# A streamed factorization-machine kernel: the columns in blocks of 512, 384 and 128 instead of 512, 352 and 160

## The reference

```python
x_reg = input_data @ W_lin.T + b_lin
emb = input_data @ factors                                   # 12500 x 16
sum_squared = jnp.square(emb.sum(axis=1))
squared_sum = (jnp.square(input_data) @ jnp.square(factors)).sum(axis=1)
h = jax.nn.relu(emb @ W1.T + b1)                             # 128
h = jax.nn.relu(h @ W2.T + b2)                               # 64
dnn_out = h @ W3.T + b3
x = x_reg + 0.5 * (sum_squared - squared_sum)[:, None] + dnn_out
x = 0.5 + jax.nn.sigmoid(x) * 5.0
```

## Time and profile before

| | |
|---|---|
| median of three runs | 133.88 us |
| time of the profiled execution | 133.76 us |
| its span in the trace | 132.0 us |
| TensorE busy (PE) | 107.0 us, 81% |
| ACT busy | 61.5 us, 47% |
| DVE busy | 52.6 us, 40% |
| DMA | 52.36 MB, mean 397 GB/s |
| chain that ended last | DMA 54%, PE 40% |

### The profile page before, as it was taken

The page is one execution under the profiler, slowest core; times in us unless marked ns, Lnnn a source line. Parts: engine busy times, 40 slices in busy tenths (PEclk is TensorE's granted clock), DMA queues, the critical chain, the costliest instruction groups (busy, mean ns, idle before and its releaser), DMA issues.

```text
span 132.0 us, 2607 instructions
## 1 busy us (share of the span) xinstructions
PE 107.0 (81%) x1123; PEld 34.6 (26%) x1123; DVE 52.6 (40%) x51; ACT 61.5 (47%) x52; POOL 15.7 (12%) x48
## 2 busy tenths in 40 slices
PE   6099969429979839749749979999998987989992
PEld 4012222002212112112112233322222112345881
DVE  0391063027036036046045016565351351576571
ACT  4030067029039039049048046868562561465851
POOL 3015000200010200200200110164530000000000
PEclk9999999995999999999977999999999999999999
DMA  3999899989999998998999999899999999999700
GB/s 106 413 531 417 377 477 472 407 387 467 427 387 462 457 427 387 457 437 387 467 457 427 387 457 447 377 432 412 452 407 407 462 415 417 418 404 411 302 26 1
DMA packets 3489, 52.36 MB, mean 397 GB/s; under 512 B 404, under 2 KB 536, under 8 KB 1560
## 3 DMA queue, kind: packets, MB, share of 16 engines
q1 hardware_dynamic: 3480, 52.23, 93.2%
HBM read 52.22 MB, written 0.00 MB: 396 GB/s over the span
## 4 chain that ended last, share of the span: by engine, by line
DMA 54%; PE 40%; SPq 2%; DVE 1%; issue 1%; ACT 1%
DMA xr<-in_x_pairs 43%; PE p_lin L506 34%; DMA xr<-in_x_end 11%; PE p_sq L506 2%; PE p_h L601 2%; SPq L273 1%; PE p_tot L506 1%; PE p_h L632 1%; PE p_tot L614 0%; DVE h L454 0%; DVE h L449 0%; SPq L267 0%; SPq L266 0%; PE p_tot L621 0%; SPq L265 0%
## 5 line engine op out<-in xcount | busy, mean ns | idle before, releaser
L327 ACT ACTIVATE sq<-xr 128x2560 f32<-128x2560 f32 x20 | 45.9, 2333 | 46.8 <-DMA xr<-in_x_pairs 38.8
L427 DVE TENSOR_TENSOR sq<-xr 128x1536 f32<-128x1536 f32 x20 | 34.6, 1761 | 53.7 <-DMA xr<-in_x_pairs 42.9
L506 PE MATMUL p_lin<-xr,wr 128*17 128x512 f32 x320 | 39.9, 638 | 15.6 <-DMA xr<-in_x_pairs 14.4
L506 PE MATMUL p_lin<-sq,wz 128*18 128x512 f32 x320 | 37.7, 592 | 0.0
L506 PEld LDWEIGHTS p_lin<-xr,wr 128*17 128x17 f32 x320 | 9.2, 102 | 44.5 <-issue 38.4
L307 POOL COPY wr<-hd 128x136 f32 (+1 forms) x20 | 9.3, 464 | 75.0 <-PE p_lin L506 75.0
L506 PEld LDWEIGHTS p_lin<-sq,wz 128*18 128x18 f32 x320 | 10.1, 98 | 25.8 <-issue 25.0
L506 PE MATMUL p_lin<-xr,hd 128*17 128x352 f32 (+1 forms) x128 | 10.0, 380 | 1.3 <-DMA xr<-in_x_end 1.3
L437 DVE TENSOR_TENSOR sq<-xr 128x1408 f32<-128x1408 f32 (+3 forms) x6 | 6.6, 1135 | 6.1 <-DMA xr<-in_x_end 6.1
L337 ACT ACTIVATE sq<-xr 128x1408 f32<-128x1408 f32 (+3 forms) x6 | 5.7, 983 | 6.3 <-DMA xr<-in_x_end 6.3
L506 PE MATMUL p_lin<-sq,ws 128*18 128x352 f32 x64 | 6.6, 459 | 0.0
(11 more groups left out here) (52 smaller groups left out, 40.8 us busy)
## 6 DMA issues: line engine op xcount, KB each, us to landing
xr<-in_x_pairs SPq DMA_DIRECT2D x8, 4096.0 KB, 21.9
xr<-in_x_groups SPq DMA_DIRECT2D x4, 2048.0 KB, 18.3
xr<-in_x_end SPq DMA_DIRECT2D x1, 2112.0 KB, 10.5
xr<-in_x_end SPq DMA_DIRECT2D x3, 640.0 KB, 12.0
xr<-in_x_end SPq DMA_DIRECT2D x1, 1760.0 KB, 14.3
xr<-in_x_end SPq DMA_DIRECT2D x1, 1056.0 KB, 12.4
hd<-in_head SPq DMA_DIRECT2D x1, 952.0 KB, 4.8
xr<-in_x_end SPq DMA_DIRECT2D x1, 704.0 KB, 13.7
```

The costliest lines, as they stand in the source:

```text
L327: nc.scalar.activation(sq[:, ring(s), BY_DVE:CHUNKS, :], xr[:, s, BY_DVE:CHUNKS, :], ACT.Square).then_inc(act_squared, 1)
L427: nc.vector.tensor_tensor(sq[:, ring(s), 0:BY_DVE, :], xr[:, s, 0:BY_DVE, :], xr[:, s, 0:BY_DVE, :], ALU.mult).then_inc(dve_squared, 1)
L506: return nc.tensor.matmul(out, lhsT, rhs, start=False, stop=False, skip_group_check=True)
```

## The change

The columns are cut into 512, 384 and 128. The first two blocks are now both done in 12 groups of 8 chunks; the groups of block 1 are 384 wide (1.57 MB), ten of them loaded as five pairs and two singly. Block 2 is 128 wide and is done over all 96 chunks in eight pieces of 24, 20, 16, 12, 8, 8, 6 and 2 chunks. In block 1 the products take their weights from the resident tables (`w`, and `ws`, which grows from 32 to 96 chunks), so POOL copies no weights there. Block 1 is closed in one go between its last group and the first piece of block 2. The bytes loaded are the same, and so is the number of products times their columns.

```diff
-ENDS = 32
+ENDS = ALL - 1
-TOTAL = 2 * GROUPS - END_GROUPS
-PAIRED = 16
+TOTAL = 2 * GROUPS
+PAIRED = TOTAL - TWO
-BLOCKS = ((0, 512), (512, 352), (864, 160))
+BLOCKS = ((0, 512), (512, 384), (512 + 384, 128))
-PIECES = ((1, 0, (4, 2), (4, 2)), (1, 12, (4, 1), (4, 1)), (1, 22, (3,), (3,)), (1, 28, (2,), (2,)),
-          (2, 0, (2, 2), (2, 2)), (2, 8, (2, 2), (2, 2)), (2, 16, (2, 2), (2, 2)), (2, 24, (2, 1), (2, 1)),
-          (2, 30, (1,), (1,)))
+PIECES = ((0, (7, 6), (6, 5)), (24, (6, 5), (5, 4)), (44, (5, 4), (4, 3)), (60, (4, 3), (3, 2)),
+          (72, (2, 2), (2, 2)), (80, (2, 2), (2, 2)), (88, (2, 1), (2, 1)), (94, (1,), (1,)))
...
+        def slots_free(i):
+
+            return TOTAL - SLOTS + TWO * ((ends_at(i) - 1) // (TWO * SLOT) + 1)
...
+                    sp.dma_start(group_chunks(TWO * p, 0, TWO * CHUNKS),
+                                 x_pairs1[p - GROUPS // TWO, :, 0:TWO * CHUNKS * WIDTH]
+                                 ).then_inc(x_landed[at // TWO], 16)
...
-            for g in range(GROUPS, TOTAL):
-                place(g, g, 1 + CHUNKS * (g - GROUPS))
...
+            act.wait_ge(sq_used, RING + TOTAL)
             copy_lin(1, 0)
             copy_lin(1, 1)
             nc.scalar.copy(rest[:, :], p_lin[1][:, BLOCKS[1][1]:HALF]).then_inc(rest_copied, 1)
             embedding_square(1)
-            square_end(4, 1)
             layer1(1, BLOCKS[1][1])
...
+            square_end(0, 0)
+            square_end(0, 1)
             sigmoid(1)
+            for i in range(1, len(PIECES)):
+                for j in range(len(PIECES[i][1])):
+                    square_end(i, j)
...
+            layer2(1)
             square_end(0, 0)
             square_end(0, 1)
+            scale(1)
+            for i in range(1, LAST_PIECE):
+                for j in range(len(PIECES[i][2])):
+                    square_end(i, j)
...
+            def multiply1(g):
+                c0 = CHUNKS * (g - GROUPS)
+                for c in range(CHUNKS):
+                    add_mm(quad(p_lin[1], c, LIN, 0, WIDTH), w[:, 1 + c0 + c, :], group_chunks(g, c, 1))
...
             first_layer(p_h1[0], BLOCKS[1][1], lin[:, cols(1)]).then_inc(p_h1_done[1], 1)
             linear(1)
             embedding_square(1)
-            multiply_end(5)
-            dve_squares_end(5, 0)
             pe.wait_ge(h1a_ready[1], 1)
             layer2(1)
-            act_squares_end(4, 1)
-            multiply_end(6)
...
+            multiply_end(0)
             layer3(1)
-            add_squares_end(6)
+            add_squares_end(0)
+            for i in range(1, LAST_PIECE - 1):
+                multiply_end(i)
+                add_squares_end(i)
+            multiply_end(LAST_PIECE - 1)
+            multiply_end(LAST_PIECE).then_inc(p_lin_done, 1)
+            add_squares_end(LAST_PIECE - 1)
             pe.wait_ge(lin_ready[2], 1)
 
             pe.wait_ge(h1b_ready[0], 1)
             first_layer(p_h1[1], BLOCKS[2][1], lin[:, cols(2)]).then_inc(p_h1_done[2], 1)
-            add_squares_end(7)
 
             pe.wait_ge(sg_ready[0], 1)
             embedding_sum(2)
-            add_squares_end(8).then_inc(squares_done, 1)
+            add_squares_end(LAST_PIECE).then_inc(squares_done, 1)
```

More of the change, by code:

```diff
@@ L203, in tot_bank, with group, group_chunks, group_squares @@
             return p_tot[k % 2]
[L205 to L225, removed]
+        x_row = xr[:, :].rearrange("p s c b -> p (s c b)")
+        sq_row = sq[:, :].rearrange("p s c b -> p (s c b)")
+        SLOT = CHUNKS * HALF
+        WIDTH = BLOCKS[1][1]
+        LAST_WIDTH = BLOCKS[LAST][1]
+        def group(g):
+            return TWO * SLOT * (g // TWO % (SLOTS // TWO)) + g % TWO * CHUNKS * WIDTH
+        def group_chunks(g, c, n):
+            at = group(g) + c * WIDTH
+            return x_row[:, at:at + n * WIDTH]
+        def group_squares(g, c, n):
+            at = SLOT * ring(g) + c * WIDTH
+            return sq_row[:, at:at + n * WIDTH]
+        def piece(c, n):
+            return x_row[:, c * LAST_WIDTH:(c + n) * LAST_WIDTH]
+        IN_RING = PIECES[4][0]
+        LAST_PIECE = len(PIECES) - 1
+        def squared_piece(c, n):
+            if c < IN_RING:
+                return sq_row[:, c * LAST_WIDTH:(c + n) * LAST_WIDTH]
+            at = group(PAIRED) + (c - IN_RING) * LAST_WIDTH
+            return x_row[:, at:at + n * LAST_WIDTH]
         def ring(s):
@@ L256, in act_count, with dve_count @@
         def act_count(i, j):
+            return sum(len(q[1]) for q in PIECES[:i]) + j + 1
+        def dve_count(i, j):
             return sum(len(q[2]) for q in PIECES[:i]) + j + 1
-        def dve_count(i, j):
-            return sum(len(q[3]) for q in PIECES[:i]) + j + 1
         @block.sync
@@ L647, in _ @@
                 for s in range(0, SLOTS, TWO):
-                    pair(r, s, 0)
+                    landed(pe, r, s)
+                    multiply(r, s, 0)
+                    multiply(r, s + 1, 0)
+                    add_squares(r, s, 0)
+                    add_squares(r, s + 1, 0)
             layer1(0)
@@ L658, in _ @@
             layer3(0)
+            pe.wait_ge(ws_ready, 2)
             for g in range(GROUPS, PAIRED, TWO):
-                pair(g // SLOTS, g % SLOTS, 1)
+                landed(pe, g // SLOTS, g % SLOTS)
+                multiply1(g)
+                multiply1(g + 1)
+                add_squares1(g)
+                add_squares1(g + 1)
             for g in range(PAIRED, TOTAL):
                 single(pe, g)
[L664 to L672, removed]
-            multiply_end(4)
-            act_squares_end(4, 0)
-            dve_squares_end(4, 0)
-            dve_squares_end(4, 1)
+                multiply1(g)
+                add_squares1(g)
             pe.wait_ge(lin_ready[1], 2)
@@ L762 @@
     params[:, C_B3] = np.asarray(L0_rec_b3)
-    arrays = {"head": head, "x_first": x_first, "x_rest": x_rest, "x_pairs": x_pairs, "x_groups": x_groups, "x_end": x_end}
+    arrays = {"head": head, "x_first": x_first, "x_rest": x_rest, "x_pairs": pairs[0], "x_pairs1": pairs[1],
+              "x_groups": x_groups, "x_end": x_end}
     nc = bacc.Bacc("TRN2", target_bir_lowering=False, num_devices=1)
```

180 lines of the change are left out of this document (75 added, 105 removed).

## The result

The changed kernel takes 137.61 us (median of four runs, 137.27 to 140.73) against 133.84: the ratio is 1.027, 95% interval 1.024 to 1.031. It is slower, as forecast, but by 3.8 us where 0.85 were forecast, and it lies above the range of 133.7 to 136.3. One of the four runs (140.73) was in a slower state that some executions of any kernel show; the ratio leaves it out. The profiled execution took 137.27 us against 133.76, its span is 135.5.

The account below looks back on a forecast made before the run. The DMA stream (54% of the chain) was taken to bound the kernel, TensorE (40%) close behind. Block 2's addition +0.98 and tail -0.13 gave +0.85 on 133.76: 134.6, or 134.7 by the median; range 133.7 to 136.3 us.

Parts of the forecast that it names:

- the tail: From block 2's addition to the last result: the same chain at 128 for 160 columns, 0.13 us less.
- Block 2 on TensorE: Block 2's products: data products end at 127.7, the addition comes at 128.0 against 127.04, 0.98 us later.
- 184 x 0.0537 = 9.9 us: In block 2, 96 data and 88 square products before the last data product's end, each priced by its 128 columns.
- The price of 160 columns: Rival in block 2: narrow products cost 0.0675 us each, as at 160 columns; 2.5 us more, 137.2 us; 3%.
- The stream did not set the end: Rival at the end: closing and backlog about 1.0 us quicker, addition follows the last landing, 133.6 us; 12%.
- nor come faster: Rival on the data stream: shorter rows load 3% faster, end at 133.6 us, or 132.7 at 5%; 12%.
- A fall of the clock on the path: Rival on TensorE: new idle before 104.15 or after 114.45 us halves its clock once, costing 1.56 us, 136.2; 10%.
- The closing term: Block 1's closing, now alone before block 2: TensorE idle 1.7 us between 114.45 and 117.6 us.

Follow-up runs that it names:

- shifted: The kernel before with 64 tiny matmuls on TensorE in its idle time ahead of group 19: 133.81 us, ratio 1.000.
- two variants: The changed kernel with block 1's closing put in between piece 0, all data loaded: 138.02 us; and with pieces 1, 2 and 3 as one piece: 138.53 us.
- The interleaved variant: The changed kernel nearly without data for pieces 1 to 7, block 1's closing in between piece 0, sigmoid and scaling behind piece 1's squares: median 134.33 us.
- with 32 and with 64 tiny matmuls: The changed kernel with 32 or 64 one-column matmuls on TensorE ahead of the last pair of block 1: 137.59 and 136.72 us.
- the kernel with merged pieces: The changed kernel with pieces 1, 2 and 3 loaded as one piece of 48 chunks, rows of 24 KB: 138.53 us.

## Why the prediction was wrong

**What held.** The bound (TensorE late after the closing, the stream no longer setting the end), the landings (group 23 at 111.53, forecast 111.45), the copies at 114.90 (114.9), piece 0 on TensorE at 117.54 (117.6), 27.3 ns a record (26.9), DVE's squares ready just as they are wanted, and the tail: from addition to last result 2.77 us, forecast 2.83. With the data of the last pieces away the whole comes to 134.58, against the forecast 134.7.

**The step that failed** is in "Block 2 on TensorE": "184 x 0.0537 = 9.9 us", with TensorE issuing without a pause. The price of a product was right. What it left out is that the instructions themselves must be loaded, by DMA beside the data: it put the two gaps, 2.66 us, at nothing. 128-column records use up a block of 256 instructions in 128 x 27.3 ns = 3.5 us, three such blocks lie nearly end to end, and where TensorE stood still beside the stream the next block was there 4.6 to 6.7 us after the one before was entered. The experiments show each part: the gap moves with the count, record by record; it goes when the stream goes; and in the kernel before a block at the same place lasts about 4.5 us, the stream ending in it, or over 6 when shifted.

I bounded the price of a narrow product by an issue cost per instruction (the 16 ns records of the earlier trace rows). Those were 24 records in a burst, too few to cross a boundary, so they could say nothing on how long such a rate can be kept up. The profile before held the hint: seven packets of 16 KB on the queue of the instructions, and near the end, from 122.9 us on, stretches in which 120 records take 4.0 us.

```profile
q8 instruction: 7, 0.11, 0.4%
```

**The rivals.** The price of 160 columns (137.2, 3%) is nearest in time, but by another mechanism: at 27.3 ns a record it is refuted. The stream did not set the end, nor come faster. A fall of the clock on the path did not happen in the profiled execution; in the profiles of two variants it came, 1.7 us each, behind a fetch gap in one and behind a wait for a landing in the other, so that rival is real, with other idle times as its source than I named. A range up to 136.3 had no case in it for a cost that no row of before shows.

**The closing term.** I gave it 1.7 us of idle time, of which 1.0 was to come back with the closing moved. The interleaved variant had 0.6 us back in the trace, and no gain clear of noise in the times. So the term is seen in one trace, and its size is known only to that.

**Which part of the change costs what.** By the profiled executions 3.5 us in sum (137.27 - 133.76): 2.7 from late instructions (137.27 - 134.55), which come from the order, narrow blocks in a row beside the stream; 0.8 from TensorE's lateness, of which the closing is perhaps 0.6. No variant was faster than the kernel before.

## What to carry to other kernels

Before cutting work into narrower matmuls beside a full stream, divide: 128 fp32 MATMUL records with their loads are one 16 KB packet of instructions, and where TensorE stood still here it took 4.6 to 6.7 us beside the stream to have the next. Without the stream it is an estimated 2.6 to 3.6 us: 0.2 to 1.2 to the packet, and 2.4 from there. If 128 records run shorter than that for more than one block, expect TensorE to starve, with no wait named in the profile but "issue". Put the narrow work where the stream is over, or mix it with wide products as the kernel before does. To tell such a gap from others, add a few dozen idle instructions upstream and see whether it moves by their number.

## What the runs showed of the hardware

- A gap in TensorE "<-issue" in mid-run, at multiples of 256 instructions, to the record: ten gaps in six kernels with narrow products beside the stream (0.86 to 2.27 us as the profile counts it). Not at every such boundary: the first one with 32 and with 64 tiny matmuls had none, nor had the kernel with merged pieces.
- The instruction packet begins 0.2 to 1.2 us after its block is entered without data traffic, and 1.1 to 4.2 beside the pieces; where TensorE stood still, the products go on 2.4 to 2.6 us after it begins.
- 128-column fp32 records with a weight load each, four strips side by side, come every 27.3 ns, for over 10 us on end without the stream. That is 0.21 ns a column, as at 160 columns (34 ns) and at 512 (3.44 us for 32 records): no time of their own shows for the weight loads.
- The granted clock fell to 0.50 within 0.4 to 0.8 us after idle times of 2.01 and 2.06 us on TensorE, and did not after 2.20 and 2.27.
